# A graph network's first two stages on one core: one-hots moved to ScalarE, scatter-adds moved behind the gathers, fewer index waits

## The chip, the cores and the metric

The kernel runs on one core of a Trainium2 chip. The metric is the device time of one execution in microseconds (us). Three executions of the kernel before took 3460.28, 3463.08 and 3467.24 us, median 3463.08. TensorE (PE) multiplies matrices, VectorE (DVE), ScalarE (ACT) and GpSimd (POOL) compute elementwise, and SyncE (SP) issues loads and stores. POOL here also issues all indirect DMAs: transfers whose 128 rows are picked by a list of indices.

## The reference, cut to what matters

A graph has 3125 nodes with 32 features, and 100000 edges sorted by destination. Four layers follow each other, each on the normalized node features and added to them.

```
agg = segment_sum(edge_attr_32, src)              # layer 0: edge features summed by source node
x += batchnorm(relu([h, agg] @ W1.T + b1)) @ W2.T + b2
x += out.at[dst].add(message(h[src], edge))       # layer 1: a message per edge, summed by destination
x += propagate(h, edges, weights, 3 rounds)       # layer 2: sparse matrix, clipped
x += propagate_normalized(h, edges, 3 rounds)     # layer 3: edge counts, with batchnorm
```

Layers 2 and 3 use the same edges again and again, so the kernel builds two dense matrices from them, one entry (count, weight) per pair of nodes, in the first two stages, beside layers 0 and 1.

## The kernel before, in words

Edges are cut into chunks of 128. There are 784 chunks (CH), 782 of them with edges (USED), in 196 steps of four chunks (STEPS). The program writes out one instruction stream per engine; the order on each is as the code has it, and semaphores alone join them.

**The first stage** (`phase0` on each engine, some 50 to 977 us) runs layer 0's sum over all 196 steps. A one-hot matrix of a chunk, 128 edges by 640 positions, is multiplied by the chunk's edge features times a second, coarser one-hot (`prod0`, line 1320). ScalarE makes a one-hot in two passes, Square (line 668) and Relu (line 673, one pass for all of a step); VectorE in one, `is_equal` (line 1311). `by_act` (line 383) says which of a step's four chunks are ScalarE's: one chunk, in every fourth step two. There are two buffers, so ScalarE's second pass waits until TensorE has used the step before the last (`s_sum[0]`). Four steps make the unit `u`; in it two groups of four chunks are also compared for repeated keys: ScalarE compares (lines 643 and 648) in odd steps, TensorE and VectorE hand flags to and fro (lines 885 to 899, 1249, 1297), and VectorE writes the merged entries and their rows in the big matrix (`group_entries`, lines 1257 to 1262, which raises `s_idx` by 2 for a group of four chunks).

**The adds.** For each chunk POOL adds the 128 merged entries into the dense matrix `both` in HBM by an indirect DMA (`add`, line 585). An add waits for its index (`s_idx`), for the add two before (`s_add[c % 2]`), and, from chunk 392 on and for even chunks, also for the add just before. POOL first stores zeros over the matrix (line 573); it waits for these, then adds chunks 0 to 391 while the first stage runs and after it.

**Between the stages** (977 to 1023 us) layer 0's dense part runs, and a table of node features is stored to HBM (line 459, SP).

**The second stage** (`phase1`, 1064 to 2818 us) runs layer 1. In each step POOL gathers the table's rows of four chunks (`gather`, line 593, two buffers, waiting for `s_terms` of the step before the last), VectorE makes the messages (lines 1433 to 1471) and products (line 1290), ScalarE all four one-hots, TensorE the sums. The entries of the chunks 392 to 783 are merged two per step here (`entries` and `entry_places`, lines 1276 to 1283), and POOL adds two chunks per step, two steps behind (BEHIND).

POOL's order in the second stage is: `gather(0)`, and then for each step s `gather(s + 1)` and, from s = 2 on, two adds. When all adds have landed and the last sums are done, SP loads the matrix (line 505) for the layers 2 and 3, which end the program.

Of the kernel before, what the change touches and what calls it, by code (L numbers as in the profile page):

```python
# [30 lines left out]
CH = -(-EDGES // (16 * P)) * 16  # L31
STEPS = CH // 4
USED = -(-EDGES // P)
# [14 lines left out]
BEHIND = 2  # L48
# [31 lines left out]
BANKS = NA // BANK_D  # L80
SPLITS = ((0, 5), (5, 15), (15, NA))
EARLY = 13
OUTS = ((0, 13), (13, NA))


# [6 lines left out]
def gnn_program(nc, x_in, src_in, dst_in, srcT_in, dstT_in, ea3_in, ea32_in, ew_in, ewT_in,  # L92
                w1T_in, b1_in, gamma_in, beta_in, w2T_in, b2_in, l1w1_in, l1b1_in, l1w2_in, l1b2_in,
                gam3_in, bet3_in, out):
    with ExitStack() as ctx:
# [3 lines left out]
        def sem(name):  # L99
            return ctx.enter_context(nc.semaphore(name))  # L100
# [196 lines left out]
        s_idx = sem("scatter_rows_ready")  # L297
# [84 lines left out]

        def by_act(k4):

            return (0, 1) if k4 == 3 else (0,)

        def half_used(r, k, half):

# [14 lines left out]
        def _(sp):  # L403
# [125 lines left out]

            for i, (a0, a1) in enumerate(OUTS):  # L530
                sp.wait_ge(s_fin, i + 1)
# [7 lines left out]
        @block.gpsimd  # L539
        def _(pool):  # L540
            def setup_tiles():

                pool.memset(ident[:, :], 0.0).then_inc(s_const, 1)
                pool.memset(earlier[:, :], 1.0).then_inc(s_const, 1)
                pool.memset(valid[:, :], 1.0).then_inc(s_const, 1)
                pool.wait_ge(s_const, 3)
                pool.affine_select(out=ident[:, :], in_=ident[:, :], compare_op=ALU.not_equal, fill=1.0,
                                   base=0, pattern=[[-1, P]], channel_multiplier=1).then_inc(s_const, 1)

                pool.affine_select(out=earlier[:, :], in_=earlier[:, :], compare_op=ALU.is_gt, fill=0.0,  # L550
                                   base=0, pattern=[[1, P]], channel_multiplier=-1).then_inc(s_const, 1)

                pool.affine_select(out=valid[:, :], in_=valid[:, :], compare_op=ALU.is_gt, fill=0.0,
                                   base=NODES, pattern=[[-P, NA]], channel_multiplier=-1).then_inc(s_const, 1)
                pool.iota(iota_b[:, :], [[1, PARTS * P]], base=0, channel_multiplier=0,
                          allow_small_or_imprecise_dtypes=True).then_inc(s_const, 1)
                pool.iota(iota_a[:, :], [[1, HI]], base=0, channel_multiplier=0,
                          allow_small_or_imprecise_dtypes=True).then_inc(s_const, 1)
                pool.iota(spare[:, :], [[P, 4]], base=BIG, channel_multiplier=1,
                          allow_small_or_imprecise_dtypes=True).then_inc(s_const, 1)  # L560

                pool.iota(node_ids[:, :, 0], [[P, NA]], base=0, channel_multiplier=0,
                          allow_small_or_imprecise_dtypes=True).then_inc(s_const, 1)
                pool.iota(node_ids[:, :, 1], [[0, NA]], base=0, channel_multiplier=1,
                          allow_small_or_imprecise_dtypes=True).then_inc(s_const, 1)

            pool.memset(zeros[:, 0:NA * ROW], 0.0).then_inc(s_zero, 1)
            pool.wait_ge(s_zero, 1)
            pool.dma_start(both[BIG:BIG + 4 * P, :].rearrange("(p c) o -> p (c o)", p=P),
                           zeros[:, 0:8]).then_inc(s_zeroed, 16)  # L570
            size = BIG // ZERO_PIECES
            for t in range(ZERO_PIECES):
                pool.dma_start(both[t * size:(t + 1) * size, :].rearrange("(p i c) o -> p i (c o)", p=P, i=2),
                               zeros[:, 0:size // P].unsqueeze(1).broadcast_to([P, 2, size // P])).then_inc(s_zeroed, 16)
                if t == 3:
                    setup_tiles()

            def add(c):

                pool.wait_ge(s_idx, c // 2 + 1)  # L580
                if c >= CH // 2 and c % 2 == 0:
                    pool.wait_ge(s_add[1], 16 * (c // 2))
                if c >= 2:
                    pool.wait_ge(s_add[c % 2], 16 * (c // 2))
                pool.indirect_dma_start(both, bass.IndirectOffsetOnAxis(ap=sc_idx[:, c:c + 1], axis=0),  # L585
                                        sc_val[:, c // 2, c % 2, :], None, compute_op=ALU.add).then_inc(s_add[c % 2], 16)

            def gather(s, ks):

                if s >= 2:  # L590
                    pool.wait_ge(s_terms, 2 * (s - 1))
                for k in ks:
                    pool.indirect_dma_start(gath[:, s % 2, k, :], None, feat_dram,  # L593
                                            bass.IndirectOffsetOnAxis(ap=src_i[:, 4 * s + k:4 * s + k + 1], axis=0)
                                            ).then_inc(s_gath[s % 2], 16)

            pool.wait_ge(s_zeroed, 16 * (ZERO_PIECES + 1))
            pool.wait_ge(s_zeroed, 16 * (ZERO_PIECES + 1))
            for c in range(CH // 2):
                add(c)  # L600
            pool.wait_ge(s_feat, 16)
            gather(0, range(4))
            for s in range(STEPS + BEHIND):
                if s + 1 < STEPS:
                    gather(s + 1, range(min(4, USED - 4 * (s + 1))))
                if s >= BEHIND:
                    for c in range(2 * (STEPS + s - BEHIND), min(2 * (STEPS + s - BEHIND) + 2, USED)):
                        add(c)


            eighths = both[0:TABLE, :].rearrange("(s d) o -> s (d o)", d=EIGHTH)
            pool.wait_ge(s_ridx, 1)
            for e in range(8):
                if e >= 2:
                    pool.wait_ge(s_over, e - 1)
                pool.indirect_dma_start(over_in[:, e % 2, :], None, eighths,  # L616
                                        bass.IndirectOffsetOnAxis(ap=row_idx[:, e:e + 1], axis=0),
                                        ).then_inc(s_overin[e % 2], 16)
# [225 lines left out]
        def _(pe):  # L844
# [206 lines left out]
            def count_round(r, opening):  # L1051
# [10 lines left out]
                def add_block(s, ds_):  # L1062

                    if opening:
                        if s < IN_KEPT:
                            pe.wait_ge(s_kept[s // 2], 16)
                        else:
                            pe.wait_ge(s_ringc[(s - IN_KEPT) // 2], 16)
                    for d in ds_:
                        pe.matmul(place(d), counts(s)[:, d * P:(d + 1) * P], parts(s),  # L1070
                                  start=(s == 0 and d % BANK_D == 0), stop=False, skip_group_check=True)
# [7 lines left out]

                for s in range(EARLY):  # L1080
                    for i, (a0, a1) in enumerate(SPLITS):
# [9 lines left out]
                for b in range(BANKS):  # L1091
                    for s in range(EARLY, NA):
                        add_block(s, range(b * BANK_D, (b + 1) * BANK_D))
# [49 lines left out]
        def _(dve):  # L1143
# [402 lines left out]
            def split_z(r=None):  # L1546

                for a0, a1 in SPLITS:
                    if r is not None:
                        normal(r, a0, a1)  # L1550
                    z, rest, to = zn[:, a0:a1, :], zrest[:, 0:a1 - a0, :], zparts[:, a0:a1, :, :]
                    link(V.tensor_tensor(z, h[:, a0:a1, :],
                                         dinv[:, 1, a0:a1].unsqueeze(2).broadcast_to([P, a1 - a0, FEAT]), ALU.mult))
                    link(V.tensor_copy(to[:, :, :, 0], z))
                    link(V.tensor_tensor(rest, z, to[:, :, :, 0], ALU.subtract))
                    link(V.tensor_copy(to[:, :, :, 1], rest))
                    link(V.tensor_tensor(rest, rest, to[:, :, :, 1], ALU.subtract))
                    V.tensor_copy(to[:, :, :, 2], rest).then_inc(s_z, 1)
# [24 lines left out]
            def normal(r, a0, a1):  # L1583

                n = a1 - a0
                link(V.tensor_tensor(h[:, a0:a1, :], cen[:, a0:a1, :],
                                     fsum[:, 4, :].unsqueeze(1).broadcast_to([P, n, FEAT]), ALU.mult))
                link(V.tensor_tensor(h[:, a0:a1, :], h[:, a0:a1, :],
                                     bet3[:, r - 3, :].unsqueeze(1).broadcast_to([P, n, FEAT]), ALU.add))
# [6 lines left out]
            for r in range(3, 6):  # L1596
# [28 lines left out]
                if r < 5:  # L1625
                    split_z(r)
            for a0, a1 in OUTS:
                normal(5, a0, a1)
# [49 lines left out]
```

## Time and profile before

| What | Value |
|---|---|
| Median of three executions | 3463.08 us |
| The profiled execution, its own time | 3467.37 us |
| Span of the profiled execution, first to last instruction | 3465.3 us |
| Busy: TensorE, VectorE, ScalarE, POOL | 2974.6, 2742.9, 2280.7, 2141.3 us |
| POOL's adds (line 585) | 782, busy 1333.0 us, mean 1705 ns |
| POOL's gathers (line 593) | 782, busy 760.8 us, mean 973 ns |
| VectorE's first-stage one-hots (line 1311) | 539 |

The rows further down come from one profiled execution. Its own time is 2.1 us over its span and 4.3 over the median. "Idle before" is time in which an engine did nothing ahead of an instruction, and the name after the arrow is what ended it; "issue" there means that the profile shows nothing that it waited for. Adjacent instructions of one engine may overlap by some hundredths of a us in the rows.

### The profile page before, as it was taken

Reading aid. Unit: us, or ns where it says so; the run is one execution under the profiler, and the core shown is the slowest. Engines: PE = TensorE matmul, PEld = TensorE weight load, DVE = VectorE, ACT = ScalarE, POOL = GpSimd, SP = SyncE. Lnnn points to the kernel's source line nnn. Section 1 sums busy time; section 2 is a strip of 40 time slices with the busy share of each in tenths; the row PEclk is TensorE's granted clock in tenths of the full one; section 3 lists DMA queues with packets and bytes.
Section 4 is the critical chain, followed back from the end, with each engine's and each line's share of the span. In section 5 each row is a group of like instructions: output and inputs, shape, how many; then the busy total and the mean of one; then the engine's idle time right before and its main releaser. Section 6 shows DMA issues by size and latency. Waiting matters only on the chain. (4 is left out here: it accounts for less than half of the span.)

```text
span 3465.3 us, 69301 instructions
## 1 busy us (share of the span) xinstructions
PE 2974.6 (86%) x19703; PEld 2370.4 (68%) x19703; DVE 2742.9 (79%) x6018; ACT 2280.7 (66%) x3192; POOL 2141.3 (62%) x1629
## 2 busy tenths in 40 slices
PE   3888788988856999999999999999999976657657
PEld 3677677777745888888888888888888851113257
DVE  6678988888856999999999999999999973441065
ACT  3678688888836888888888888888888842220000
POOL 4048888888877777777777777777777730000000
PEclk9899899999977999999999999999999997798778
DMA  9943222222222333333333333333333359998940
GB/s 400 419 154 38 12 15 15 15 16 16 15 25 41 53 53 52 50 53 51 50 53 51 50 53 51 51 53 52 50 53 52 50 187 426 426 391 342 373 172 6
DMA packets 265695, 388.67 MB, mean 112 GB/s; under 512 B 149903, under 2 KB 200838, under 8 KB 259254
## 3 DMA queue, kind: packets, MB, share of 16 engines
q0 software_dynamic: 149184, 120.78, 20.7%
q1 hardware_dynamic: 100034, 195.42, 16.6%
q10 hardware_dynamic: 16416, 71.74, 5.1%
q8 instruction: 28, 0.46, 0.1%
q14 instruction: 33, 0.27, 0.0%
HBM read 260.01 MB, written 127.78 MB: 112 GB/s over the span
## 5 line engine op out<-in xcount | busy, mean ns | idle before, releaser
L585 POOL DMA_INDIRECT both<-kept x782 | 1333.0, 1705 | 439.8 <-issue 194.6
L923 PEld LDWEIGHTS ps<-prod,big 128*128 128x128 f32 x7840 | 1133.9, 190 | 137.7 <-DVE prod L1290 133.0
L923 PE MATMUL ps<-prod,big 128*128 128x170 f32 x7840 | 1183.2, 310 | 22.5 <-DVE prod L1290 17.4
L593 POOL DMA_INDIRECT kept<-feat_dram,kept x782 | 760.8, 973 | 243.2 <-issue 233.1
L668 ACT ACTIVATE big<-iota_b,kept 128x640 f32<-128x640 f32 x1029 | 779.0, 815 | 13.6
L914 PE MATMUL ps<-prod,onehot 128*128 128x320 f32 x3920 | 684.5, 325 | 81.2 <-DVE prod L1320 79.6
L914 PEld LDWEIGHTS ps<-prod,onehot 128*128 128x128 f32 x3920 | 597.7, 194 | 112.9 <-DVE prod L1320 84.5
L673 ACT ACTIVATE big<-big 128x2560 f32<-128x2560 f32 x196 | 458.0, 2337 | 277.2 <-PE ps L923 277.1
L988 PE MATMUL ps<-w2mix,kept 65*128 65x384 f32 x1568 | 559.3, 500 | 21.7 <-ACT kept L720 20.4
L1462 DVE TENSOR_REDUCE kept<-kept 128x80 f32<-128x1280 f32 x392 | 561.4, 1471 | 0.0
L988 PEld LDWEIGHTS ps<-w2mix,kept 65*128 65x128 f32 x1568 | 284.2, 191 | 179.7 <-issue 25.5
L1452 DVE TENSOR_TENSOR kept<-ps,kept 128x384 f32<-128x384 f32 x784 | 395.3, 544 | 0.0
L616 POOL DMA_INDIRECT prod<-both,row_idx x8 | 7.8, 977 | 526.2 <-DVE row_idx L1570 512.4
L1320 DVE TENSOR_TENSOR prod<-kept 128x1280 fp32r<-128x1280 f32 x196 | 291.9, 1489 | 4.3
L1311 DVE TENSOR_SCALAR onehot<-iota_b,kept 128x640 fp32r<-128x640 f32 x539 | 291.4, 593 | 0.0
L673 ACT ACTIVATE onehot<-big 128x640 fp32r<-128x640 f32 x196 | 171.1, 873 | 182.4 <-PE ps L914 173.7
L1129 PE MATMUL ps<-big,zring 128*32 128x512 f32 (+3 forms) x400 | 183.5, 615 | 118.6 <-DMA big<-both 106.8
L1448 DVE TENSOR_TENSOR kept<-ps,kept 128x512 f32<-128x512 f32 x392 | 266.1, 679 | 0.0
L643 ACT ACTIVATE kept<-ps,kept 128x128 f32<-128x128 f32 (+2 forms) x588 | 223.3, 477 | 0.0
L1129 PEld LDWEIGHTS ps<-big,zring 128*32 128x32 f32 x400 | 45.3, 124 | 256.8 <-issue 242.3
L1520 DVE TENSOR_REDUCE row_max<-big 128x1 f32<-128x1600 f32 x50 | 91.0, 1819 | 160.0 <-DMA adj_c<-kept 107.6
L765 ACT ACTIVATE kept<-big 128x1600 f32<-128x1600 f32 x50 | 82.2, 1648 | 187.0 <-issue 83.2
(235 smaller groups left out, 3028.9 us busy)
## 6 DMA issues: line engine op xcount, KB each, us to landing
both<-big POOLq DMA_DIRECT2D x40, 1910.0 KB, 91.2
big<-both SPq DMA_DIRECT2D x24, 1600.0 KB, 11.8
big<-both SPq DMA_DIRECT2D x24, 1528.0 KB, 13.2
kept<-keys_dram SPq DMA_DIRECT2D x196, 128.0 KB, 3.0
kept<-in_wT SPq DMA_DIRECT2D x196, 128.0 KB
adj_c<-kept ACTq DMA_DIRECT2D x42, 400.0 KB, 31.6
kept<-adj_c SPq DMA_DIRECT2D x9, 1600.0 KB, 22.4
adj_w<-kept ACTq DMA_DIRECT2D x16, 800.0 KB, 33.6
```

The source lines that it names most:

```text
L585: pool.indirect_dma_start(both, bass.IndirectOffsetOnAxis(ap=sc_idx[:, c:c + 1], axis=0), sc_val[:, c // 2, c % 2, :], None, compute_op=AL ...
L593: pool.indirect_dma_start(gath[:, s % 2, k, :], None, feat_dram, bass.IndirectOffsetOnAxis(ap=src_i[:, 4 * s + k:4 * s + k + 1], axis=0)). ...
L668: act.activation(dist[:, k, :], iota_b[:, :], ACT.Square, scale=-1.0, bias=bcol[:, ds(4 * s + k, 1)]).then_inc(s_dist[n], 4 // len(ks))
L673: act.activation(to[:, q, 0:len(ks), :], dist[:, 0:len(ks), :], ACT.Relu, scale=-1.0, bias=1.0).then_inc(s_oh[n], 1)
L914: mm = pe.matmul(ps[:, SUM0[part], 0:HI * 2 * FEAT], onehot0[:, q, k, part * P:(part + 1) * P], prod0[:, q, k, :, :].rearrange("p a m -> p ...
L923: mm = pe.matmul(part_sums(part, MSG), onehot[:, q, k, part * P:(part + 1) * P], prod[:, q, k, 0:HI * MSG], start=False, stop=False, skip_ ...
L988: mm = pe.matmul(ps[:, 4 + k, 0:384], hidT[:, q, k * P:(k + 1) * P], w2mix[:, :], start=True, stop=True)
L1311: ins = V.tensor_scalar(onehot0[:, q, k, :], iota_b[:, :], b_src[:, ds(4 * s + k, 1)], None, ALU.is_equal)
L1320: V.tensor_tensor(prod0[:, q, :, :, :], high0[:, ds(4 * s, 4), :].unsqueeze(3) .broadcast_to([P, 4, HI, 2 * FEAT]), rows0[:, 4 * k4:4 * k4 ...
L1448: V.tensor_tensor(T[:, :, 0:256].rearrange("p k (o x) -> p k o x", o=16), ps[:, 4 + 2 * g:6 + 2 * g, 0:256].rearrange("p k (o x) -> p k o ...
L1452: ins = V.tensor_tensor(T[:, k, 256:640].rearrange("p (u i x) -> p u i x", u=8, i=3), ps[:, 4 + 2 * g + k, 256:384].rearrange("p (u x) -> ...
L1462: V.tensor_reduce(res[:, q, 2 * g:2 * g + 2, 0:40], terms[:, g, :, :].rearrange("p k (o x) -> p k o x", x=16), AX, ALU.add).then_inc(s_red, 1)
```

## The change: what it does

ScalarE makes two one-hots in the steps 0 and 2 of four, and one in the steps 1 and 3. POOL makes 372 adds ahead of the first gather, not 392. In the loop over steps it makes a pair of adds in every step from s = 0 on, as far as the old bound of two steps behind allows, and in every sixteenth step (s % 16 = 15) a pair ahead of the gathers as well. An add of the first 392 chunks waits for its index in every fourth chunk alone, for the whole group; a later one in every second chunk, for the pair.

```diff
+AHEAD, MIX = 372, 16
...
         def by_act(k4):
-            return (0, 1) if k4 == 3 else (0,)
+            return (0, 1) if k4 % 2 == 0 else (0,)
...
             def add(c):
-                pool.wait_ge(s_idx, c // 2 + 1)
+                if c < CH // 2 and c % 4 == 0:
+                    pool.wait_ge(s_idx, c // 2 + 2)
                 if c >= CH // 2 and c % 2 == 0:
+                    pool.wait_ge(s_idx, c // 2 + 1)
                     pool.wait_ge(s_add[1], 16 * (c // 2))
                 if c >= 2:
                     pool.wait_ge(s_add[c % 2], 16 * (c // 2))
...
-            for c in range(CH // 2):
+            for c in range(AHEAD):
                 add(c)
+            added = AHEAD
+            def add_pair(s):
+                c = min(added + 2, USED, 2 * (STEPS + s - BEHIND) + 2)
+                for i in range(added, c):
+                    add(i)
+                return max(added, c)
             pool.wait_ge(s_feat, 16)
             gather(0, range(4))
             for s in range(STEPS + BEHIND):
+                if s % MIX == MIX - 1:
+                    added = add_pair(s)
                 if s + 1 < STEPS:
                     gather(s + 1, range(min(4, USED - 4 * (s + 1))))
-                if s >= BEHIND:
-                    for c in range(2 * (STEPS + s - BEHIND), min(2 * (STEPS + s - BEHIND) + 2, USED)):
-                        add(c)
+                added = add_pair(s)
+            for c in range(added, USED):
+                add(c)
```

## Rows read from the trace of the kernel before

**Rows 1.** The page: POOL's busy tenths in 40 slices of 86.6 us.

```profile
POOL 4048888888877777777777777777777730000000
```

**Rows 2.** Groups on POOL, 1100 to 2790 us: count | busy us, mean ns | idle before.

```profile
L593 POOL DMA_INDIRECT kept<-feat_dram,kept x753 | 732.5, 973 | 229.5 <-issue 225.8 <-DMA both<-kept 3.7
L585 POOL DMA_INDIRECT both<-kept x378 | 614.5, 1626 | 115.2 <-issue 65.2 <-DVE kept L1283 50.0
```

**Rows 3.** Waits, 1100 to 2790 us: who <- for whom, total us, times, longest.

```profile
POOL kept L593 <- issue: 225.8, 741, 0.3
...
DVE kept L1433 <- DMA kept<-feat_dram,kept: 33.1, 119, 0.4
```

**Rows 4.** Timeline of VectorE at the second stage's end: start us, duration, the instruction.

```profile
2797.49 0.26 DVE L1433 TENSOR_TENSOR kept<-kept 128x96 f32<-128x96 f32 x1
...
2805.94 0.25 DVE L1433 TENSOR_TENSOR kept<-kept 128x96 f32<-128x96 f32 x1
```

**Rows 5.** The table in HBM (feat_dram): its store, and issue to landing.

```profile
L459 SPq DMA_DIRECT2D feat_dram<-big x1: 383/383/383, 1023.3 to 1023.3; - x1
...
DMA to landing us min/median/max: 6.4/6.4/6.4
```

**Rows 6.** Timeline of POOL where adds give way to gathers.

```profile
1011.80 1.54 POOL L585 DMA_INDIRECT both<-kept  x1 [0.80 <-DMA both<-kept]
...
1030.88 1.54 POOL L585 DMA_INDIRECT both<-kept  x1 [4.15 <-DMA both<-kept]
...
1057.58 1.02 POOL L593 DMA_INDIRECT kept<-feat_dram,kept  x1 [0.30 <-issue]
```

**Rows 7.** Timeline of VectorE, first instruction of the second stage.

```profile
1063.94 0.28 DVE L1433 TENSOR_TENSOR kept<-kept 128x96 f32<-128x96 f32 x1 [40.63 <-DMA kept<-feat_dram,kept]
```

**Rows 8.** Timelines of VectorE and TensorE over four steps of the first stage.

```profile
714.91 1.49 DVE L1320 TENSOR_TENSOR prod<-kept 128x1280 fp32r<-128x1280 f32 x1
...
718.04 1.53 DVE L1311 TENSOR_SCALAR onehot<-iota_b,kept 128x640 fp32r<-128x640 f32 x3
...
722.90 0.16 DVE L1297 TENSOR_SCALAR kept<-ps 128x1 bf16<-128x1 f32 x1 [0.64 <-PE ps L899]
...
712.97 1.74 PE L914 MATMUL ps<-prod,onehot 128*128 128x320 f32 x10 [1.38 <-DVE prod L1320]
...
721.09 1.73 PE L914 MATMUL ps<-prod,onehot 128*128 128x320 f32 x10 [0.25 <-DVE prod L1320]
```

**Rows 9.** Line 1308, once per four steps, by stretch: busy us (count), clock, DMA.

```profile
60.00:212.00 152.00, 2.99 (x7) 0.88 0.96 395
...
420.00:970.00 550.00, 13.53 (x31) 1.00 0.25 15
```

**Rows 10.** Timeline of ScalarE in the first stage: a square, two second passes.

```profile
711.96 0.81 ACT L668 ACTIVATE big<-iota_b,kept 128x640 f32<-128x640 f32 x1
...
716.80 0.74 ACT L673 ACTIVATE onehot<-big 128x640 fp32r<-128x640 f32 x1 [2.28 <-PE ps L914]
...
722.77 1.27 ACT L673 ACTIVATE onehot<-big 128x1280 fp32r<-128x1280 f32 x1
```

**Rows 11.** POOL's adds: their group, 213 to 1013 us; index waits, 200 to 980.

```profile
L585 POOL DMA_INDIRECT both<-kept x372 | 668.0, 1796 | 304.4 <-DMA both<-big 171.0 <-issue 121.3 <-DMA both<-kept 10.1
...
POOL both L585 <- DVE kept L1262: 2.0, 2, 1.7
```

**Rows 12.** Timeline of POOL, two adds of the first stage.

```profile
715.16 2.66 POOL L585 DMA_INDIRECT both<-kept  x1 [0.30 <-issue]
718.12 1.54 POOL L585 DMA_INDIRECT both<-kept  x1 [0.30 <-issue]
```

**Rows 13.** Groups on POOL, 1058 to 1100 us: the gathers of the first steps.

```profile
L593 POOL DMA_INDIRECT kept<-feat_dram,kept x24 | 23.5, 979 | 12.2 <-DVE kept L1452 6.1 <-issue 5.8 <-DMA both<-kept 0.3
```

**Rows 14.** Timeline of POOL at the second stage's end: pairs of adds without gathers between.

```profile
2808.48 1.56 POOL L585 DMA_INDIRECT both<-kept  x1 [2.26 <-DMA both<-kept]
...
2814.07 1.80 POOL L585 DMA_INDIRECT both<-kept  x1 [2.19 <-DMA both<-kept]
```

## The prediction

> **What bounds the kernel now.** I read the busy digits of the page first. POOL is busy in eight tenths of every slice of the first stage from 212 us on and in seven tenths of the second [rows 1]. That looks like slack, but every POOL instruction has a fixed pause in front of it that is not counted as busy. So the second view is POOL's groups over the steady second stage, 1100 to 2790 us [rows 2]: 753 gathers busy 732.5 us and 378 adds busy 614.5 us, with 229.5 and 115.2 us of idle time before them. Together 1691.7 us of a 1690 us stretch: POOL has no free time. The pause is no wait for data: 225.8 us over 741 gathers is 0.305 us each, and 0.3 is also the longest [rows 3]. Gathers of a step's second to fourth chunk wait for no semaphore at all, adds for two or three, and all have the same pause; a wait that is already met costs POOL nothing there.
>
> Is VectorE bound as well? It waits for gathers 119 times, 33.1 us in all [rows 3]. Where nothing was late, at the end of the stage, a VectorE step took 2805.94 - 2797.49 = 8.45 us [rows 4], against 8.98 on POOL: 6 pauses of 0.305, 4 gathers of 0.973 and 2 adds of 1.626 make 8.97 [rows 2]. **The second stage goes at POOL's pace**, and so does the start: table data are ready at 1029.7 (store issued at 1023.3, landed 6.4 later [rows 5]), but POOL works off its adds until the first gather at 1057.58 [rows 6], and VectorE stands 40.63 us [rows 7]. POOL is one serial chain from 212 to 2818 us, 782 adds and 782 gathers. The change removes none of them; it reorders them.
>
> **First stage, one-hots.** Per four steps VectorE makes 10 instead of 11, ScalarE 6 instead of 5. VectorE loses one in step 0 and one in step 2, and takes one more in step 3. One in a train of three costs 1.53 / 3 = 0.51 us, and 0.49 in the cleaner trains, which I take. TensorE stands 1.38 us for step 0's products and 0.25 for step 2's [rows 8]. Step 2 can give back its 0.25 only. Step 3's extra one-hot falls into a VectorE wait for TensorE of 0.64 us [rows 8], which is its cover; without it, it would cost 0.49 again. Step 0 then starts 0.24 earlier and is 0.49 shorter: 0.73 us per four steps. The first stage has 49 such groups; 31 run in 550 us, 17.74 us each, and only 7 in the 152 us under the zeroing, 21.7 each, where other waits cover the saving [rows 9]. With 40 groups that gain, the stage ends 40 x 0.73 = 29 us earlier. Ends of the range: 0, if TensorE and ScalarE take it all back, and 46 if ScalarE's own work were the only limit. ScalarE gains one square of 0.81 and a wider second pass, 1.27 for 0.74: 1.34 us more, and it now idles 2.28 in front of one pass of the four steps [rows 10]. Behind that pass on its queue stand the key comparisons, whose result VectorE wants only in the next group of four chunks. So the 1.34 is hidden by the 2.28, and 17.74 - 2.28 + 1.34 = 16.80 us is ScalarE's floor (49 x 0.94 = 46, the upper end).
>
> So the table lands at about 1029.7 - 29 = 1000.7.
>
> **First stage, POOL.** The 372nd add ends at 1011.80 + 1.54 = 1013.3 [rows 6]. In that stretch 372 adds have 304.4 us idle before them, 171.0 of it the zeroing ahead of the first [rows 11]; 133.4 less 371 x 0.305 leaves 20.2 us. Little of it is an index wait (2.0 over two adds); what else is named is the landing of the add two before (10.1) [rows 11]. Dropping three of four index waits removes a wait that is nearly always met, but leaves the landing wait as the only one on those adds. Bounds: nothing (met waits cost nothing in the second stage) and 20.2; I take 10, because the late landings themselves remain. An add in the stage takes 1796 ns [rows 11] against 1540 clean; with the stage ending 29 us earlier some 14 adds more run clean, about 3 us. The table's store made one add wait 4.15 us [rows 6]; that store now falls into the ahead adds: 3.9 us back. The 372nd add ends at 1013.3 - 10 - 3 + 3.9 = 1004.2, after the table landed: **gathers start at 1004, 53.4 us earlier.**
>
> Is the 1796 made by one-hots? The add at 718.12 ran inside a train of three (718.04) and took a clean 1.54; the add at 715.16 started inside the step's product (714.91, 1.49 long) and took 2.66 [rows 8, 12]. So products, of which there are as many as before, stretch adds, and I take nothing for the missing one-hot. The Trainium skill, page "SBUF — State Buffer", section "Who interferes with whom", says otherwise of the one-hots: a tensor_scalar in a 2-port mode shuts GpSimd out of the shared port for its whole length. By that rule one eleventh of 372 x 0.256 = 95 us would go, an estimate of 8.7 us, the table would be the later one and the sum below would be -0.6 in place of 2.9; the clean add inside a train speaks against it.
>
> **Second stage.** It gets 20 adds more, at 0.305 and 1.54 to 1.63 each: 38 us; before, they took 1057.58 - 1013.34 = 44.2 in the gap. Four of them stand in steps 0 and 1, where POOL waited for VectorE's terms: 6.1 us over four gathers, 4.9 above the pause [rows 13], now filled. The other 16 come as an extra pair ahead of a step's gathers in every sixteenth step, right behind the pair of the step before. **That adds a wait**: from chunk 392 on, the first add of a pair waits for both landings of the pair before. Twice the trace has two pairs without gathers between, at the very end, and POOL stood 2.26 and 2.19 us [rows 14], 1.93 above the pause. Behind the waiting add are the pair's second and the four gathers, and VectorE behind these. The sixteenth steps are 12; the pair is displaced in the last four too, though nothing is owed any more: 12 x 1.93 = 23.2 us. Below 0 a wait can't go, and 2.3 each is the upper end. Dropping the odd add's index wait gains nothing by the flat pause.
>
> **Sum.** -53.4 + 38 + 23.2 - 4.9 = +2.9 us at the end of the second stage; what follows starts from it and is untouched. The profiled execution took 3467.37 us (span 3465.3), 4.3 above the median 3463.08 of the three runs; 3470.3 on its base, **3466.0 us on the median's**. A measurement of this kernel can tell some 0.2% (7 us) from no change, so this is no change. Case 1, POOL's chain conserved, holds from -4 to +12 us (3459 to 3475): chance 0.56, of which 0.38 same, 0.16 slower, 0.02 faster.
>
> **Rivals.** Case 2, slower: the first stage does not shorten, since TensorE or ScalarE becomes its limit, and POOL stands idle after add 372 for the table. It decides when the stage gains less than 25 us; at 10 us gathers start at 1019.7 and the sum is +18.6, at 0 it is +28.6. For it: TensorE waits only 1.63 us in four steps [rows 8]. Against: the 0.73 is inside that. Chance 0.18.
>
> Case 3, faster: the landing waits nearly all go (20 us for 10) and the stage gains 45. Add 372 ends at 994, or 990 without the meeting with the store: -7 to -11. For: the rows don't name the cause of most of the 20. Against: in the second stage a met wait costs nothing [rows 3]. Chance 0.12.
>
> Case 4, faster: POOL's pause is partly made by VectorE's pace after all, and the 20 adds and 12 waits are half absorbed: -53.4 + 0.5 x 56.3 = -25, chance 0.14. Against: the flat 0.305, and the step of 8.45 [rows 3, 4]. That the change doesn't do what it says is within case 1: without any gain on waits the sum is +12.9.
>
> **How the numbers follow.** Faster 0.02 + 0.12 + 0.14 = 0.28; same 0.38; slower 0.16 + 0.18 = 0.34. The range leaves out the far half of case 4 and the worst of case 2: 3463 - 20 = 3443 to 3463 + 26 = 3489.
>
> **What would show it.** In the changed profile: four first-stage steps in 17.0 us; TensorE's wait of 0.25 gone; the last ahead add and the table's landing within 5 us of each other near 1000; VectorE's wait before its first step below 25 us; twelve more POOL waits of some 2.2 us on a landing; a step still at 8.97; the last gather within 12 us of where it was. I am wrong if the pause before adds falls below 0.3, if extra pairs show no wait, or if steps go under 8.9 us.

## The result and the profile after

**Slower, by 29 us.** On the same chip four executions of the changed kernel had a median of 3494.33 us (3490.58 to 3494.8), four of the kernel before 3465.16: ratio 1.0084, 95% interval 1.0066 to 1.0103. Forecast was 3466.0, range 3443 to 3489, no change. The profiled executions are closer: 3490.58 us (span 3488.5) against 3467.37, 23.2 us, since one lies 3.8 under its median and the other 2.2 over. Line numbers moved: adds are L588, gathers L596, the product L1334, a VectorE step begins at L1447.

The start went as forecast. POOL's timeline where adds give way to gathers, the table's store, VectorE's first instruction of the second stage, and the windows of the line that runs once per four first-stage steps:

```profile
991.77 1.54 POOL L588 DMA_INDIRECT both<-kept  x1 [0.30 <-issue]
996.71 1.54 POOL L588 DMA_INDIRECT both<-kept  x1 [3.41 <-DMA both<-kept]
999.00 1.54 POOL L588 DMA_INDIRECT both<-kept  x1 [0.75 <-DMA both<-kept]
...
1003.41 1.54 POOL L588 DMA_INDIRECT both<-kept  x1 [1.03 <-DMA both<-kept]
...
1007.10 1.02 POOL L596 DMA_INDIRECT kept<-feat_dram,kept  x1 [0.30 <-issue]
```

```profile
L460 SPq DMA_DIRECT2D feat_dram<-big x1: 382/382/382, 989.9 to 989.9; - x1
...
DMA to landing us min/median/max: 6.4/6.4/6.4
```

```profile
1013.47 0.29 DVE L1447 TENSOR_TENSOR kept<-kept 128x96 f32<-128x96 f32 x1 [23.58 <-DMA kept<-feat_dram,kept]
```

```profile
420.00:930.00 510.00, 13.40 (x30) 1.00 0.25 16
```

Four steps take 510 / 30 = 17.0 us, where they took 17.74 [rows 9]; the table lands at 996.3 instead of 1029.7 [rows 5], the first gather goes out 50.5 us earlier [rows 6]. VectorE waits 23.58 us for it instead of 40.63 [rows 7]. POOL's 372 adds ahead, 213 to 1006 us:

```profile
L588 POOL DMA_INDIRECT both<-kept x372 | 666.7, 1792 | 299.2 <-DMA both<-big 171.9 <-issue 116.5 <-DMA both<-kept 10.7
```

299.2 - 171.9 - 371 x 0.305 = 14.1 us of pauses above the fixed one, against 20.2 [rows 11]. Of these 14.1 the three waits beside the table's store above are 3.41 + 0.75 + 1.03 - 0.9 = 4.3. (0.9 is three fixed pauses.)

Then the second stage gives it back. POOL's groups, 1060 to 2790 us, and the waits, 1100 to 2790 us:

```profile
L596 POOL DMA_INDIRECT kept<-feat_dram,kept x742 | 728.9, 982 | 226.1 <-issue 223.4 <-DMA both<-kept 2.7
L588 POOL DMA_INDIRECT both<-kept x388 | 631.0, 1626 | 143.1 <-issue 96.3 <-DMA both<-kept 28.1 <-DVE kept L1297 18.6
```

```profile
DVE kept L1447 <- DMA kept<-feat_dram,kept: 81.2, 58, 6.4
...
POOL both L588 <- DMA both<-kept: 28.1, 11, 3.1
```

Eleven adds waited 28.1 us on a landing; before [rows 2, 3] adds had no such wait there. A gather has grown from 973 to 982 ns, and VectorE waits for gathers 58 times, not 119, but up to 6.4 us instead of 0.4. One extra pair on POOL's timeline, its first add held by the pair right ahead of it:

```profile
1146.13 1.65 POOL L588 DMA_INDIRECT both<-kept  x1 [0.30 <-issue]
1150.16 1.56 POOL L588 DMA_INDIRECT both<-kept  x1 [2.38 <-DMA both<-kept]
1152.02 1.54 POOL L588 DMA_INDIRECT both<-kept  x1 [0.30 <-issue]
1153.87 1.38 POOL L596 DMA_INDIRECT kept<-feat_dram,kept  x1 [0.30 <-issue]
```

There are twelve such pauses, 2.24 to 3.15 us long, the last at 2792.02. What that one does to VectorE, each time the first instruction of a step:

```profile
2786.83 0.25 DVE L1447 TENSOR_TENSOR kept<-kept 128x96 f32<-128x96 f32 x1
...
2802.18 0.26 DVE L1447 TENSOR_TENSOR kept<-kept 128x96 f32<-128x96 f32 x1 [6.56 <-DMA kept<-feat_dram,kept]
...
2810.89 0.30 DVE L1447 TENSOR_TENSOR kept<-kept 128x96 f32<-128x96 f32 x1
...
2820.93 0.25 DVE L1447 TENSOR_TENSOR kept<-kept 128x96 f32<-128x96 f32 x1
...
2829.44 0.24 DVE L1447 TENSOR_TENSOR kept<-kept 128x96 f32<-128x96 f32 x1
```

One step lasts 15.35 us, and the stage ends before VectorE has caught up. Its last step starts 23.5 us later than before (2805.94 [rows 4]); the last gather ends at 2820.8, which is 18.4 later.

### The profile page after: what moved, and what is told of

Its sections match the earlier page's. It is cut to its first block and busy times, and to the rows that moved or that the text cites. A ratio compares the mean times of both kernels' runs of the same rounds, so it can differ in the third digit from the quotient of the medians.

```text
span 3488.5 us, 68811 instructions
## 1 busy us (share of the span) xinstructions
PE 3014.6 (86%) x19702; PEld 2413.2 (69%) x19703; DVE 2727.2 (78%) x5969; ACT 2344.0 (67%) x3241; POOL 2148.3 (62%) x1629
## 5 line engine op out<-in xcount | busy, mean ns | idle before, releaser
L588 POOL DMA_INDIRECT both<-kept x782 | 1332.5, 1704 | 457.0 <-issue 218.6
L937 PEld LDWEIGHTS ps<-prod,big 128*128 128x128 f32 x7840 | 1165.3, 194 | 125.6 <-DVE prod L1304 117.2
L937 PE MATMUL ps<-prod,big 128*128 128x170 f32 x7840 | 1207.9, 315 | 23.4 <-DVE prod L1304 19.2
L596 POOL DMA_INDIRECT kept<-feat_dram,kept x782 | 768.4, 983 | 238.3 <-issue 235.3
L682 ACT ACTIVATE big<-iota_b,kept 128x640 f32<-128x640 f32 x1078 | 814.7, 816 | 13.6
L1002 PE MATMUL ps<-w2mix,kept 65*128 65x384 f32 x1568 | 585.5, 519 | 31.3 <-ACT kept L734 20.3
L1002 PEld LDWEIGHTS ps<-w2mix,kept 65*128 65x128 f32 x1568 | 293.5, 197 | 200.6 <-issue 43.3
L1334 DVE TENSOR_TENSOR prod<-kept 128x1280 fp32r<-128x1280 f32 x196 | 292.4, 1492 | 4.0
L1325 DVE TENSOR_SCALAR onehot<-iota_b,kept 128x640 fp32r<-128x640 f32 x490 | 258.7, 577 | 0.0
L687 ACT ACTIVATE onehot<-big 128x1280 fp32r<-128x1280 f32 x196 | 197.3, 1006 | 84.6 <-PE ps L928 66.4
```

The source lines that it names most:

```text
L682: act.activation(dist[:, k, :], iota_b[:, :], ACT.Square, scale=-1.0, bias=bcol[:, ds(4 * s + k, 1)]).then_inc(s_dist[n], 4 // len(ks))
L687: act.activation(to[:, q, 0:len(ks), :], dist[:, 0:len(ks), :], ACT.Relu, scale=-1.0, bias=1.0).then_inc(s_oh[n], 1)
L937: mm = pe.matmul(part_sums(part, MSG), onehot[:, q, k, part * P:(part + 1) * P], prod[:, q, k, 0:HI * MSG], start=False, stop=False, skip_ ...
L1002: mm = pe.matmul(ps[:, 4 + k, 0:384], hidT[:, q, k * P:(k + 1) * P], w2mix[:, :], start=True, stop=True)
L1325: ins = V.tensor_scalar(onehot0[:, q, k, :], iota_b[:, :], b_src[:, ds(4 * s + k, 1)], None, ALU.is_equal)
L1334: V.tensor_tensor(prod0[:, q, :, :, :], high0[:, ds(4 * s, 4), :].unsqueeze(3) .broadcast_to([P, 4, HI, 2 * FEAT]), rows0[:, 4 * k4:4 * k4 ...
```

## The experiments

Theory A is the serial chain of POOL: the pauses of the twelve extra pairs, and the pairs displaced after nothing is owed, are what costs. Its rival B: moving adds among the gathers costs by itself, or TensorE's clock does, since it falls after each extra pair (last section). "Chain" is the time from the start of the first gather to the end of the last: 1744.8 us before, 1813.7 after. Each ratio is to the kernel before on the same chip. The stretch ahead of the gathers varies: in the first two kernels below it has the same instructions and ends 8.5 us apart (adds of 1816 and 1792 ns), so the chain, which is 1744.3 to 1747.2 us in every run with the old order, is the better witness.

**Extra pair between the gathers.** The same pairs, with two gathers in front of each extra pair:

```diff
+chunks = range(min(4, USED - 4 * (s + 1)))
 if s % MIX == MIX - 1:
+    gather(s + 1, chunks[:2])
     added = add_pair(s)
-if s + 1 < STEPS:
-    gather(s + 1, range(min(4, USED - 4 * (s + 1))))
+    gather(s + 1, chunks[2:])
+elif s + 1 < STEPS:
+    gather(s + 1, chunks)
```

> The extra pair of every sixteenth step stands between the second and the third gather, not right behind the pair of the step before; all else as changed. Theory A (POOL is one serial chain and the twelve waits on a landing are what was mis-sized): the twelve pauses of 2.2 to 3.2 us (31 us in all in the changed kernel) go back to 0.3 each, the last gather comes 26 to 29 us earlier, at 2792 to 2795, and the time is about 28 us below the changed kernel's, 0.998 to 1.002 of the time before. Theory B (the 20 moved adds and the loss of TensorE's clock after each extra pair cost the time, whatever the pauses): no more than 8 us below the changed kernel, 1.006 or more of the time before.

Measured: 3468.83 us, ratio 1.0022 (1.0010 to 1.0035); chain 1789.0. POOL's timeline at an extra pair, and its gathers, 1060 to 2770 us:

```profile
1157.15 0.98 POOL L596 DMA_INDIRECT kept<-feat_dram,kept  x1 [0.30 <-issue]
1158.79 1.61 POOL L588 DMA_INDIRECT both<-kept  x1 [0.66 <-issue]
1160.70 1.58 POOL L588 DMA_INDIRECT both<-kept  x1 [0.30 <-issue]
```

```profile
L596 POOL DMA_INDIRECT kept<-feat_dram,kept x745 | 732.7, 984 | 227.0 <-issue 225.8 <-DMA both<-kept 1.2
```

The two gathers cover the landing; no pause above 0.66 is left, and 24.7 us of the chain go with them. As many adds are moved, so B in its first form falls. The time is just past A's 1.002, since the first gather went out 7.9 us later than in the changed kernel. The longer gathers (984) stay, and so does VectorE's lateness: its last step starts 9.7 us after the last gather's end, 8.7 in the changed kernel and 3.6 before.

**No extra pair once nothing is owed.**

```diff
-if s % MIX == MIX - 1:
+if s % MIX == MIX - 1 and s < 128:
```

> Extra pairs in steps 15 to 127 alone, where adds are owed; the four later ones, which only displace the step's own pair, are gone. Theory A: four pauses less (2.5 to 3.2 us each, 11 us), and VectorE is not behind at the end of the stage (5 us): 14 to 17 us below the changed kernel, about 1.004 of the time before. Theory B (the catch-up costs, not the displaced pairs): within 4 us of the changed kernel.

Measured: 3474.92 us, 1.0037 (1.0018 to 1.0055); chain 1799.3. Waits 1060 to 2770 us, gathers 1100 to 2790 us:

```profile
POOL both L588 <- DMA both<-kept: 20.2, 8, 2.7
```

```profile
L596 POOL DMA_INDIRECT kept<-feat_dram,kept x732 | 712.3, 973 | 223.1 <-issue 220.3 <-DMA both<-kept 2.7
```

Eight pauses are left and the gathers are back at 973 ns. VectorE's last step starts at 2809.4, 20.0 us earlier than in the changed kernel, for four pairs that I had priced at 7.7.

**Both together.**

> The changed kernel with the extra pairs between the second and the third gather, and in steps 15 to 127 alone. Theory A: no pause on a landing, VectorE not behind at the end; gathers start at 1006 to 1015, the chain of the second stage is 1745 + 38 - 4 = 1779 to 1784 us, the last gather ends at 2787 to 2798, the time is 0.995 to 0.999 of before. Theory B (the loss of TensorE's clock after each extra pair costs time): clock still falls eight times, and the time is 1.000 or above.

Measured: 3458.66 us, 0.9982 (0.9968 to 0.9997); chain 1781.9, pauses above the fixed one 0.7 us in all. The adds are still moved and TensorE's clock still falls, eight times: B falls in both forms.

**Extra pair every eighth step.**

```diff
-AHEAD, MIX = 372, 16
+AHEAD, MIX = 372, 8
```

> The changed kernel with an extra or displaced pair in every eighth step: 24 in place of 12, each right behind the pair of the step before. Nothing is added or left out; the 20 owed adds are caught up by step 63. Theory A: twelve pauses more of 2.3 to 2.8 us above the usual one, 28 to 34 us, the time 1.015 to 1.019 of before. Theory B (the pauses are absorbed elsewhere, the clock or the moved adds cost): within 10 us of the changed kernel, below 1.012.

Measured: 3521.75 us, 1.0167 (1.0145 to 1.0190); chain 1838.4. Waits, 1060 to 2770 us:

```profile
POOL both L588 <- DMA both<-kept: 50.3, 21, 3.3
```

The chain exceeds that of before, plus 38.4 us for the 20 adds more (table below), by 55.2 us instead of 30.5, so the cost nearly doubles with the pairs, as A has it. The time is up also by a first gather that went out 9.5 us later than in the changed kernel, which is not the pairs' doing.

**New one-hots and waits, old order.**

```diff
-AHEAD, MIX = 372, 16
+AHEAD, MIX = 392, 16
...
-                if s % MIX == MIX - 1:
-                    added = add_pair(s)
```

> The one-hots and the index waits of the change, with all 392 adds ahead of the gathers and no extra pairs. Theory A: adds end some 11 us earlier than before, since the first stage is quieter for longer and pauses less; gathers start at about 1046, the chain of the second stage is again 1745 us, the time 10 to 14 us below before, 0.996 to 0.997. Theory B (an earlier first stage or TensorE's clock is itself what slows the second stage): 1.000 or above.

Measured: 3456.4 us, 0.9982 (0.9967 to 0.9997): a gain, a little less than forecast. Chain 1744.3, first gather at 1052.2. Without its pauses and late pairs the new order equals this one: the run of "both together" starts gathers 39.8 us earlier and needs 37.6 us more for the chain.

**New order alone**, with the old one-hots and the old waits:

> The order of the adds alone: 372 ahead and the extra pairs, with one-hots and index waits as before. Theory A: the table lands at 1030, POOL has done 372 adds at 1013 and stands 16 us for it; gathers start at 1030, the second stage's chain is 1814 us as in the changed kernel, and the time is 1.011 to 1.013 of before (about 3505). Theory B (the second stage goes at VectorE's pace and only the number of extra pairs counts): the same as the changed kernel, 1.008.

Measured: 3518.22 us, 1.0165 (1.0143 to 1.0186). POOL's timeline:

```profile
1005.42 1.54 POOL L586 DMA_INDIRECT both<-kept  x1 [0.40 <-issue]
1036.25 1.02 POOL L594 DMA_INDIRECT kept<-feat_dram,kept  x1 [29.29 <-DMA feat_dram<-big]
```

POOL stands 29.29 us for the table, which lands at 1036.0: the case that I had as the slower rival. The expectation was too low since the table came 6 us later than in the kernel before (why it did stays open) and since it left out VectorE's lateness at the end, 5 us as in the changed kernel. The pauses ahead are 20.3 us here, without the table's store among them, against 14.1 - 4.3 = 9.8 in the changed kernel, which has the new waits and the new one-hots.

**New one-hots alone.**

> The kernel before with the changed share of one-hots alone (ScalarE two in even steps, one in odd). Theory A (POOL's serial chain sets the end of the second stage): the first stage ends 29 to 33 us earlier and the table lands at about 1000, but POOL works off its 392 adds until 1050 to 1060 as before; the time stays within 0.998 to 1.002 of before. Theory C (the first stage's length is on the path): the time falls with it, 0.990 to 0.992.

Measured: 3465.99 us, 1.0010 (0.9999 to 1.0022). The first stage ends 25 us earlier (952.4 against 977.8) and the table lands at 1003.9, but the adds end at 1054.6 and the chain is 1744.8: the gain vanishes behind POOL's 392 adds. The new waits alone are what this run lacks beside that of new one-hots and waits. POOL's adds, 213 to 1054 us here and 213 to 1051 there:

```profile
L585 POOL DMA_INDIRECT both<-kept x392 | 694.7, 1772 | 319.0 <-DVE kept L1262 171.5 <-issue 128.9 <-DMA both<-kept 18.5
```

```profile
L588 POOL DMA_INDIRECT both<-kept x392 | 706.0, 1801 | 305.1 <-DMA both<-big 171.5 <-issue 123.2 <-DMA both<-kept 10.4
```

Fewer waits save 28.2 - 14.3 = 13.9 us of pauses, but the adds take 11.3 us more, and the first gather goes out only 2.6 us earlier. A pause saved is not yet time saved; why the adds are longer was not tried.

**364 adds ahead**, extra pairs between gathers every twelfth step up to 144:

> As the kernel with the pairs between the gathers and only while owed, with 364 adds ahead (28 to catch up, 12 extra pairs, one in every twelfth step). Theory A: the adds ahead end at about 991 to 998, the table lands at 996 to 998, so nothing waits for the landings that the table's store delays (4 us); 8 adds more in the second stage cost 15 us, gathers start 15 us earlier: 0 to 5 us below the kernel with 372. If the adds end well before the table, POOL stands for it and it is 0 to 5 us above.

Measured: 3464.21 us, 1.0006 (0.9995 to 1.0017).

```profile
993.97 1.55 POOL L588 DMA_INDIRECT both<-kept  x1 [0.30 <-issue]
1000.53 1.02 POOL L596 DMA_INDIRECT kept<-feat_dram,kept  x1 [5.01 <-DMA feat_dram<-big]
```

Now POOL waits for the table; fewer adds ahead than the table leaves room for cost time.

**A VectorE one-hot more in every step**, on the kernel before, into columns that nothing reads (196 more of 128x640):

```diff
+again = big[:, 0, 2400:3040]
...
+if k == 2:
+    V.tensor_scalar(again, iota_b[:, :], b_src[:, ds(4 * s + k, 1)], None, ALU.is_equal)
```

> The kernel before, with one first-stage one-hot of each step made twice by VectorE (the second copy goes to unused columns): 196 more of them, 0.49 us each. If one-hots shut POOL out for their length (the rule of the Trainium skill, page SBUF — State Buffer, section Who interferes with whom), the 392 adds ahead rise by a third of their excess, from a mean of 1784 to 1860 ns or more. If it is the products, their share of the time falls and the adds stay at 1760 to 1810 ns. Theory A: the first stage grows by up to 96 us, the table lands at 1080 to 1125, after POOL's adds, and from there each us shows: the time is 1.006 to 1.02 of before.

Measured in one execution: 3518.88 us, against 3450.66 before on that chip. POOL's adds, 213 to 1066 us, and its first gather:

```profile
L587 POOL DMA_INDIRECT both<-kept x392 | 702.5, 1792 | 322.1 <-DMA both<-big 171.1 <-issue 122.9 <-DVE kept L1264 17.9
```

```profile
1107.97 1.02 POOL L595 DMA_INDIRECT kept<-feat_dram,kept  x1 [42.50 <-DMA feat_dram<-big]
```

392 adds have a mean of 1792 ns against 1784 before: 392 x (1792 - 1540) = 99 us above a clean add, and 96 before. By this mean alone one-hots would cost the adds nothing. The single rows say otherwise: two one-hots of this run and the add that starts inside the second; then a train of three in the kernel before and the add that starts in it, just ahead of those in [rows 8, 12].

```profile
708.28 1.02 DVE L1315 TENSOR_SCALAR onehot<-iota_b,kept 128x640 fp32r<-128x640 f32 x2
```

```profile
708.86 1.85 POOL L587 DMA_INDIRECT both<-kept  x1 [0.30 <-issue]
```

```profile
712.90 1.76 DVE L1311 TENSOR_SCALAR onehot<-iota_b,kept 128x640 fp32r<-128x640 f32 x3
```

```profile
712.98 1.88 POOL L585 DMA_INDIRECT both<-kept  x1 [0.30 <-issue]
```

The first ends 1.41 us after the one-hot (710.71 - 709.30). Of the adds ahead that start 0.1 to 0.4 us after the beginning of a train, all are longer than a clean one, 8 of 8 before and 17 of 17 here; of those that start within 0.1 us of it, 38 of 57 before are clean, and the add at 718.12 [rows 12] is one of these. In the table an add counts as held by the VectorE instruction in which it starts when it ends 1.34 to 1.48 us after that instruction:

| Adds ahead, us above 1.54 (number) | Before | 196 more one-hots |
|---|---|---|
| Held by products | 54.3 (67) | 43.9 (82) |
| Held by one-hots | 11.2 (38) | 36.2 (128) |
| All adds | 95.5 | 98.6 |

So one-hots do hold adds; products and other instructions held them less in this run, and the mean hid it. Why the two nearly cancel was not tried. The rule of the Trainium skill, page "SBUF — State Buffer", section "Who interferes with whom", that the prediction weighed (a tensor_scalar in a 2-port mode shuts GpSimd out for its whole length) agrees with these rows; in which mode the one-hots run, no run here shows. The stage ends 78 us later, and now POOL waits for it.

**The product in halves, in quarters**, both on the kernel with new one-hots and waits and the old order. TensorE waits for the part that it needs. The diff is that of halves; quarters make each k an instruction of its own, and TensorE's wait is for 4 * s + k + 1:

```diff
+for k in range(0, 4, 2):
+    V.tensor_tensor(prod0[:, q, k:k + 2, :, :], ..., ALU.mult).then_inc(s_prod[0], 2)
-V.tensor_tensor(prod0[:, q, :, :, :], ..., ALU.mult).then_inc(s_prod[0], 4)
...
-                pe.wait_ge(s_prod[0], 4 * s + 4)
+                pe.wait_ge(s_prod[0], 4 * s + k // 2 * 2 + 2)
```

> As the kernel with one-hots and waits in the old order, with VectorE's first-stage product (1.49 us) in two instructions of two chunks each, and TensorE waiting for the half that it needs. Theory D (an add that starts inside a product waits for that instruction's end): half as long a product costs an add half as much, 0.25 us falls to 0.13, the mean of the 392 adds from 1800 to about 1680 ns; POOL is done with them some 40 us earlier, at 1008 to 1018, near the table's landing; the time is 0.986 to 0.992 of before. Rival: the stretch has another cause or isn't given up between two products: adds at 1780 or more, the time 0.997 or above.

> The same with the product in four instructions, one chunk each. Theory D: the excess falls to a quarter, the mean to 1610 to 1650 ns; POOL is done at 990 to 1005; VectorE pays some 0.2 us a step for the further instructions, so the table lands at 1005 to 1040 and is the later one: the time is 0.985 to 0.995 of before. Rival: as for the halves.

Measured: halves 3429.93 us, 0.9940 (0.9922 to 0.9959), short of the forecast; **quarters 3412.04 us, 0.9888 (0.9870 to 0.9906), faster than both kernels of this case.** The adds ahead in halves, then in quarters:

```profile
L588 POOL DMA_INDIRECT both<-kept x392 | 667.9, 1704 | 305.5 <-DMA both<-big 172.9 <-issue 121.2 <-DMA both<-kept 10.8
```

```profile
L588 POOL DMA_INDIRECT both<-kept x392 | 655.7, 1673 | 306.4 <-DMA both<-big 172.6 <-issue 120.0 <-DMA both<-kept 13.8
```

The mechanism came out, at a smaller size than forecast: adds of 1801, 1704, 1673 ns with one, two and four instructions. By the count above, adds held by products cost about 73, 30 and 17 us, near the half and the quarter that were forecast; those held by one-hots cost 13, 21 and 20. The forecast had put the whole excess down to the products. 392 x 0.128 = 50 us, and the first gather of quarters goes out at 1003.3 instead of 1052.2; the chain behind it is unchanged (1745.0). The two traces are from different chips; by the ratios, each to the kernel before on its own chip, quarters gain 0.9% on new one-hots and waits, some 33 us. How it works shows in single rows. In the changed kernel, VectorE's product and the add that starts inside it; then in quarters, three adds around two trains of four:

```profile
715.64 1.49 DVE L1334 TENSOR_TENSOR prod<-kept 128x1280 fp32r<-128x1280 f32 x1
```

```profile
716.33 2.21 POOL L588 DMA_INDIRECT both<-kept  x1 [0.42 <-issue]
```

```profile
717.10 1.70 DVE L1333 TENSOR_TENSOR prod<-kept 128x320 fp32r<-128x320 f32 x4
...
725.94 1.70 DVE L1333 TENSOR_TENSOR prod<-kept 128x320 fp32r<-128x320 f32 x4
```

```profile
716.61 1.54 POOL L588 DMA_INDIRECT both<-kept  x1 [0.30 <-issue]
718.53 1.68 POOL L588 DMA_INDIRECT both<-kept  x1 [0.38 <-issue]
...
726.08 1.77 POOL L588 DMA_INDIRECT both<-kept  x1 [0.34 <-issue]
```

The first ends 1.41 us after the product's end (718.54 - 717.13), as the one in [rows 8, 12] did, 1.42; the one in the train's last quarter ends 1.41 after the train (720.21 - 718.80). The one that starts in the first quarter of the next train ends only 0.21 after it (727.85 - 727.64), which is 1.41 after the first quarter's end, three quarters of some 0.4 us earlier: it did not wait for the train. The add at 716.61, under way when the train begins, is a clean 1.54. So an add that starts inside a product ends 1.41 us after that one instruction, and a shorter instruction lets it go sooner. I had expected the table at 1005 to 1040 in quarters; it landed at 976.0, since the first stage did not lengthen by its extra instructions but ended at 924.5.

## Why the prediction was wrong

Its sum, term by term, at the places where the trace can be read:

| Term, us | Forecast | Measured |
|---|---|---|
| First gather | -53.4 | -50.5 |
| 20 adds more in the second stage | +38 | +38.4 |
| Twelve landing pauses above 0.305 | +23.2 | +27.6 |
| POOL's waits in steps 0 and 1 | -4.9 | -4.9 |
| Gathers' own time (760.8 to 768.4) | 0 | +7.7 |
| End of the last gather | +2.9 | +18.4 |
| VectorE behind at the end | 0 | +5.1 |
| VectorE's last step | +2.9 | +23.5 |

**Right:** POOL as one serial chain; the first stage, 33 us earlier against 29 (944.5 for 977.8); the 10 us of pauses that fewer waits save (20.3 less 9.8 by the new order alone) and the store's 3.9 (4.3); the 0.305 as a fixed pause; the 20 adds. Case 2 did not come: the table landed 10.5 us ahead of the last add's end. That the first gather came within 3 us of the forecast is in part luck: in the five kernels with these instructions ahead of it the adds ahead end at 1006.2 to 1016.3, the changed kernel's at 1006.8.

**Wrong, without much weight in the sum:** that one-hots do not stretch adds. It was read from one add that starts 0.08 us into its train, and the rows above show others held. One-hots hold some 11 of the 95 us, so one in eleven fewer is worth about 1 us. Case 2's sums should read +18.4 and +28.4. Of the signs that were named, two failed: the last add and the table were to be within 5 us of each other, and the last gather within 12 of where it was.

**Wrong, the step on the displaced pairs:** "the pair is displaced in the last four too, though nothing is owed any more: 12 x 1.93 = 23.2 us". Two things were missed in it. A pause is 2.6 us, not 2.2; the two pairs of the tail [rows 14] were the nearest rows, but a bound drawn from two rows was too tight. And the work queued behind the pair was named ("the four gathers, and VectorE behind these") but not priced. A pair that is owed nothing pulls its two adds ahead of gathers that VectorE needs at once: at 2792.02 two adds with their fixed pauses, 3.7 us, and a landing pause 2.85 above the fixed one make the 6.56 that VectorE stands. VectorE's late steps take some 8.7 us while POOL goes at 8.97, so it wins back about 0.3 per step and after each of these pairs is late for some 14 steps; in that time gathers run longer, single ones up to 1.67 us, and after the pair of step 191 no steps are left to recover in. Without these four pairs the gathers are at 973 ns again and VectorE's last step comes 20.0 us sooner. That the longer gathers meet VectorE's products, as the adds do in the first stage, fits but was not tried by itself.

So the range was too narrow by 5 us at its upper end: case 1 went up to 12 us, with no term for what a displaced step does to the engine behind it. The part of the change that moves adds had nothing to win, as the sum said: with pauses and late pairs mended it stands where the old order stands with the same one-hots and waits, 0.9982 both.

## What to carry to other kernels

On an engine that is one serial chain, as POOL is here, moving work from one stage to another gains nothing, while each wait that the new order adds is paid in full; put independent work between two dependent pairs. Price a displaced group by how late its consumer gets and how many steps it has to recover, above all near a stage's end. When an indirect DMA is slow only beside certain VectorE instructions, look at which instruction each slow one started in, and split those into shorter ones: here that was worth 0.9%, and the reordering nothing. Do not judge by a mean over all: the adds' mean hid what the added one-hots did.

## What was not expected of the hardware

TensorE's granted clock falls after each of the twelve extra pairs; in the 13.2 us around the first one TensorE was busy 11.03 us. Windows of the changed kernel: busy times (TensorE's first), then granted clock, DMA share and rate.

```profile
1150.00:1163.20 13.20, 11.03 (x71) 9.09 (x69) 6.63 (x17) 10.63 (x14) 10.63 (x8) 0.97 0.27 35
1163.20:1173.40 10.20, 9.40 (x24) 6.44 (x25) 9.62 (x23) 4.95 (x9) 8.07 (x7) 0.53 0.33 45
1173.40:1300.00 126.60, 125.57 (x778) 106.57 (x778) 120.72 (x283) 104.22 (x140) 99.15 (x84) 1.00 0.32 51
```

At 0.53 it is near the lower of its two levels, 1.2 GHz, for 10.2 us; the kernel before has 1.00 in all three. It cost little: with the extra pairs between the gathers it still fell twelve times (3.4 to 10.2 us each) and the kernel was 0.6% faster; the second stage goes at POOL's pace.

The other surprise is that an add that starts inside a VectorE product does not run slowly beside it, it stands until the product ends: all 85 adds ahead that start in a product of the changed kernel end 1.40 to 1.56 us after that product's end. One-hots hold adds too, for a shorter time.
